# Layer 1: the two parts of the output are summed by an accumulating transfer from GpSimd's queue

## The reference, cut to what matters

```python
def _L1_conv_ref(x, ...):
    z = softplus(_involution(x, ...))            # a 3x3 kernel per pixel, made from x
    y = conv_general_dilated(z, w_conv2, (1, 1), padding=((1, 1), (1, 1)))
    y = y + b_conv2[None, :, None, None]
    return softplus(y)

# --- layer 0 ---
x = x + _L0_conv_ref(_gn(x), ...)
# --- layer 1 ---
x = x + _L1_conv_ref(_gn(x), ...)
```

## Time and profile before

| | us |
|---|---|
| median of three runs | 9394.1 |
| the profiled execution's own time | 9387.9 |
| its span, first to last instruction | 9385.9 |
| of which the stage of layer 1's strips, about | 2245 (from about 7140 on) |
| mean granted TensorE clock | 0.993 of full speed |

### The profile page before, as it was taken

One profiled execution on the slowest core, in us unless ns is written; L12 is line 12 of the kernel. 1 busy time (PEld: TensorE's weight loads), 2 busy tenths in 40 slices (PEclk: granted clock), 3 DMA queues, 4 the chain that ended last, 5 costly groups with the idle time before them and its releaser, 6 DMA issues. The chain is left out here.

```text
span 9385.9 us, 168801 instructions
## 1 busy us (share of the span) xinstructions
PE 9042.0 (96%) x58884; PEld 5002.5 (53%) x58884; DVE 6029.8 (64%) x7793; ACT 6408.4 (68%) x8676; POOL 4911.1 (52%) x2751
## 2 busy tenths in 40 slices
PE   0999999999999999999999999999987999999999
PEld 0666666666666666666666666666532333333333
DVE  4555555555555555555555555555566999999999
ACT  0676676666666666766766676676604888888888
POOL 1444444344444434444443444434305999999999
PEclk9999999999999999999999999999998999999999
DMA  6222222222222222222221212122195444444444
GB/s 142 52 49 64 49 59 59 56 59 49 64 51 58 60 54 59 49 64 49 59 59 42 50 40 50 40 50 50 34 237 121 118 118 120 120 120 119 118 119 118
DMA packets 618105, 715.18 MB, mean 76 GB/s; under 512 B 44230, under 2 KB 577196, under 8 KB 594200
## 3 DMA queue, kind: packets, MB, share of 16 engines
q1 hardware_dynamic: 618008, 713.88, 31.6%
HBM read 549.02 MB, written 164.70 MB: 76 GB/s over the span
## 5 line engine op out<-in xcount | busy, mean ns | idle before, releaser
L573 PE MATMUL banks<-w_hi,hi_lo 128*128 128x256 f16 x18432 | 2351.3, 273 | 51.7 <-DVE hi_lo L837 51.7
L573 PEld LDWEIGHTS banks<-w_hi,hi_lo 128*128 128x128 f16 x18432 | 1784.3, 98 | 456.9 <-ACT qk L716 204.5
L531 POOL TENSOR_TENSOR u_im<-q_im,k_swap 128x512 f32<-128x512 f32 x512 | 727.3, 1421 | 2103.3 <-ACT q_im L734 2031.1
L716 ACT ACTIVATE qk<-banks,inv_wscale 128x512 f32<-128x512 f32 x1024 | 704.2, 688 | 1504.6 <-PE banks L573 1491.5
L1324 POOL TENSOR_TENSOR part_sum<-part_sum,prod 128x1024 f32<-128x1024 f32 x660 | 1561.3, 2366 | 53.4 <-POOL part_sum L1324 0.4
L1353 PE MATMUL banks<-z,conv_w 128*128 128x512 f32 x3128 | 1575.1, 619 | 0.0
L846 DVE TENSOR_TENSOR u<-q_re,banks 128x512 f32<-128x512 f32 x512 | 350.9, 685 | 1483.2 <-ACT q_re L736 1475.6
L521 POOL TENSOR_TENSOR hl_all<-xn,hi_all 64x1280 f16<-64x1280 f32 x258 | 793.2, 3075 | 584.7 <-ACT hi_all L709 533.7
L590 PE MATMUL banks<-hi_lo,w_hi 128*128 128x512 f16 x4608 | 1084.1, 380 | 10.0 <-DVE tmp L915 10.0
L534 POOL TENSOR_TENSOR u<-u,u_im 128x512 f32<-128x512 f32 x512 | 651.0, 1272 | 690.7 <-DVE u L846 675.9
L573 PE MATMUL banks<-w_lo_pair,hi_pair 128*128 128x256 f16 x6144 | 1006.0, 273 | 0.0
(11 more groups left out here) (217 smaller groups left out, 15959.4 us busy)
## 6 DMA issues: line engine op xcount, KB each, us to landing
xr<-in_x_dram SPq DMA_DIRECT2D x258, 640.0 KB, 9.0
xb<-y_scratch SPq DMA_DIRECT2D x268, 320.0 KB, 4.5
xa<-y_scratch SPq DMA_DIRECT2D x268, 256.0 KB, 5.0
x_res<-in_x_dram SPq DMA_DIRECT2D x258, 256.0 KB, 3.8
out_dram<-res SPq DMA_DIRECT2D x258, 256.0 KB, 3.2
y_scratch<-ys SPq DMA_DIRECT2D x256, 256.0 KB, 3.8
yc<-y_scratch SPq DMA_DIRECT2D x256, 256.0 KB, 5.4
xs<-in_x_dram SPq DMA_DIRECT2D x92, 512.0 KB, 7.1
```

Source lines behind the costliest of these rows:

```text
L531: nc.gpsimd.tensor_tensor(u_im[:], q_im[:], k_swap[:], ALU.mult).then_inc(u_made, 1)
L573: r = pe.matmul(out, px, w, start=n == 0, stop=n == 13)
L716: act.activation(qk[:, 2 * h:2 * h + 2, :], b_qk[h][:].rearrange("p (t c) -> p t c", t=2), ACT.Copy, scale=inv_wscale[:, 0:1]).then_inc(qk ...
```

## The change

GpSimd's `tensor_tensor` that adds `ab2[b]` to `res[b]` is taken out. In its place GpSimd issues one transfer `res[b] <- ab2[b]` with `accum_op=ALU.add`: the DMA engines read both tiles and write the sum back to `res[b]`. It is issued after the first of the six sums (n = 0), no longer ahead of it; the waits ahead of the sums stay where they are. A transfer adds 16 to its semaphore when it has landed, so SP's and ACT's waits for `out_ready` count in steps of 16.

```diff
@@ blk.sync, body
-                        given_out, stored = i * 4 + (k - 2), i * 64 + 16 * (k + 2)
+                        given_out16, stored = i * 64 + 16 * (k - 2), i * 64 + 16 * (k + 2)
...
-                            given_out, stored = sp.snap(given_out), sp.snap(stored)
+                            given_out16, stored = sp.snap(given_out16), sp.snap(stored)
...
-                            sp.wait_ge(out_ready, given_out)
+                            sp.wait_ge(out_ready, given_out16)
                             store(to, (k + 1) % 2)
@@ blk.gpsimd, body
                             pool.wait_ge(log2_ready, i * 4 + (k - 2))
-                            nc.gpsimd.tensor_tensor(res[b][:], res[b][:], ab2[b][:], ALU.add).then_inc(out_ready, 1)
                         for n in range(6):
                             pool.wait_ge(prod_ready, i * 36 + (9 * k + n + 2))
...
                             nc.gpsimd.tensor_tensor(part_sum[:], prod[0][:] if n == 0 else part_sum[:], prod[n + 1][:], ALU.add)\
                                 .then_inc(pool_step, 1)
+                            if n == 0 and not (first and k < 3):
+                                nc.gpsimd.dma_start(res[b][:], ab2[b][:], accum_op=ALU.add).then_inc(out_ready, 16)
@@ blk.scalar, conv_abs
-                        act.wait_ge(out_ready, v - 1)
+                        act.wait_ge(out_ready, v * 16 - 16)
```

## The result

The changed kernel takes 9645.0 us (median of four runs, 9629.9 to 9650.4) against 9391.4 us in the runs of the kernel before beside it. The ratio is 1.027, 95% interval 1.0252 to 1.0288: slower, by 254 us. Over 129 steps that is 1.97 us a step, 18.82 in place of 16.85 us. The prediction said 9840 us, range 9500 to 10300, by the mechanism that the following rows show; its size was too large.

The account below looks back on a forecast made before the run. GpSimd's seven adds were taken to set the 16.85 us step. The new loop, 14.3 + 6.0 = 20.3 us, adds 3.45 us times 129, 445 us, to 9387.9: 9833, stated as 9840 us, range 9500 to 10300.

Parts of the forecast that it names:

- The loop: DVE's add, GpSimd's first sum, transfer, SP's queue, parts landed, PE's select: closes in one step, 14.3 + L us.
- the constant 14.3: Sum of the step's path without the transfer: 4.56, 1.23, 2.38 and 6.13 us.
- Its own signs: Prediction wrong if SP issues stores less than 3.5 us later in the step, or PE's select waits for something else.
- slack of 3.5 us: Between the parts landing at about 9022.5 and PE's select of weight 0 at 9026.02.
- L: The new transfer from issue to landing: 6.0 us taken, 3.5 to 9.0 as ends, break-even 2.55.
- One copy's price: Rival, 0.12: the adding transfer costs as one copy, landing in 3.5 us; time about 9515 us.
- The clock: Rival, 0.20: TensorE's clock falls in PE's new pauses, up to 1.5 us a step, 195 us; about 10035 us.
- Slow adder: Rival, 0.12: the transfer's adder is slower than the copy, landing in 9 us; about 10225 us.
- GpSimd standing: Rival, 0.07: GpSimd stands until its transfer has landed, its loop 21.8 us; about 10030 us.
- Faster: Rival, 0.03: landing under 2.55 us, GpSimd's loop decides, DVE's 0.35 us wait goes; 45 us less, about 9345.
- nothing changes: Rival, 0.02: landing between 2.4 and 2.7 us, or issue about 1 us with a short landing; 9395 us.
- What bounds the kernel before: GpSimd's seven adds set the step of 16.85 us, with DVE next, 0.35 us behind.

Follow-up runs that it names:

- the filler: Changed kernel with two matmuls of 0.86 us more on PE each step, ahead of the select of weight 0: 9624.2 us.
- either move: Changed kernel with the transfer issued ahead of the six sums, 9391.1 us, or with SP's wait and stores moved behind the reads of the parts, 9390.7 us.
- the first experiment: Changed kernel with the transfer issued ahead of the six sums instead of after the first one: 9391.1 us, ratio 0.9998.

## Why the prediction was right, and where it was not

- **The loop.** Right in each piece. From landing to select it said 6.13 us, the trace has 6.1; to DVE's add 4.56 against 4.47; the constant 14.3 against 14.1 to 14.3 from three transfers of different length. Its own signs held: SP issues the stores 5.8 us later in the step than before, where it asked for 3.5 or more, and PE's select waits for the parts. PE and DVE pause there by 1.7 and 2.1 us and not by the 3 to 4 foretold, since the step grew by 1.97 us and not by 3.45. Of the slack of 3.5 us some 2.3 were tried, with the transfer issued first, and cost nothing.
- **L.** This is the term that was mis-sized: 6.0 us foretold, 4.5 measured, so 445 us foretold and 254 measured. The step that failed is the line from 192 to 512 KB in the earlier trace rows, which gave 5 ns a KB over a fixed 0.9 us, and so 5.1 us for the data of both reads. Those transfers have DRAM on one side; none of them moves SBUF to SBUF. The copy of 512 KB between two SBUF tiles takes 2.9 us, not 3.5. The two adding transfers, 3.3 us for 256 KB and 4.5 for 512, give 2.4 us for the data of the whole one over a fixed 2.1. The doubling for the second read was right in engine time (1.3 to 2.8 us); it was applied to a data part that was too large. The rows were also a choice: the page of the kernel before has a third group of 512 KB, `xs<-in_x_dram`, at 7.1 us, which "the two of 512 KB" passes over.
- **The match that is left is partly luck.** With 4.5 for L the prediction's sum gives 1.95 us a step, 252 us, beside 254 measured. But the forecast put the clock at nothing, and it has some 21 to 24 us; the constant is 0.1 to 0.2 us a step smaller than its 14.3. The two errors nearly cancel.
- **One copy's price** (rival, 0.12): falls, 4.5 against 2.9 us for the copy itself. The estimate from the Trainium skill ("DMA: Bandwidth & Descriptors", Anatomy of one DMA — SWDGE (gpsimd) path), 3.2 us, is near the copy's 2.9 us and 1.3 us short for the adding transfer, for which it isn't stated.
- **The clock** (rival, 0.20): the mechanism is real and the price per event was right, 1.5 us from layer 0's row and 1.5 here. But it comes in 16 steps, not in all 129: about 24 us, not 195. What the Trainium skill says ("TensorE: Matmul & The Clock Gate", What's actually happening), that idle time gates the clock and work releases it, is borne out by the filler.
- **Slow adder, GpSimd standing:** fall. GpSimd's next sum starts 0.6 us after the issue began (9170.39 to 9171.00), long before the landing at 9174.9. Its issue takes 0.87 us, against the 0.75 taken from SP's row, and delays the next sum by 0.6.
- **Faster, nothing changes:** fall. Both needed an L under 2.7 us. The point where the time turns was read well, 2.55: the copy, at 2.9 us, still costs 0.24 us a step.
- **What bounds the kernel before.** Half right. GpSimd's adds do set the step, but the prediction set PE's 999.9 busy us of 1000 aside as modelled ends and named DVE next, 0.35 us behind. PE stands at the same 16.85 us. So the 39 to 45 us of gain, in the faster rival and in two expectations, could not come. It did not touch the forecast, where SP's loop is the longest.

No version that computes the whole result was faster than the kernel before; with either move the change costs nothing and gains nothing.

## What to carry to other kernels

Before an operation's result is handed over to a transfer, look at who waits for the result and what stands behind that wait in the same queue: here it did not matter that the stores were late, but that the six unrelated reads behind them were. Compare the landing with the slack of those, not with the time that the engine saves. And before counting on the saved time, look for a second engine without gaps: two limits at the same height make each relief alone worth nothing.

## What the hardware showed that was not expected

- An adding transfer of 512 KB between SBUF tiles from GpSimd's queue: 4.5 us to landing, 0.87 us of issue. A plain copy of the same tiles: 2.9 us and 0.57 us of issue. Half the adding transfer: 3.3 us, and its issue is no shorter, 0.87 us.
- The five sums behind the issue take 12.44 us where they took 12.14. With the issue ahead of a wait, as in the first experiment, they take 12.16. The 0.3 us is paid by the sum that overlaps the issue, 2.66 us in place of 2.37:

```profile
9189.68 2.66 POOL L1323 TENSOR_TENSOR part_sum<-part_sum,prod 128x1024 f32<-128x1024 f32 x1
```

- The transfer in flight can slow another, though here not on a path that sets the step. In the first experiment it overlaps the store of the parts, and that store lands after 2.8 us in place of 1.9; in the changed kernel the store lands by the time the transfer is issued and keeps its 1.9.
- With a pause of 1.7 us on PE in each step of 18.7 us, the clock fell to 1.2 GHz in 16 of some 129 steps; with PE's work carried into the pauses it fell in none.
